# A fused attention and FFN kernel: more of the exponential on VectorE, with other places for the FFN product and the last head

## What is computed

```
x = x + attention(layernorm(x))
  q = x Wq^T  (4 query groups x 8 heads x 16),  k, v = x Wk^T, x Wv^T  (8 heads x 16)
  a_dot = softmax(q k^T / sqrt(16)) v            # full, over the 2048 tokens of the batch
  sigma = elu(q);  a_mem = sigma memory / (sigma memory_norm)
  out   = a_dot (1 - w) + a_mem w,   w = sigmoid(memory_weight)
x = x + ffn(layernorm(x))
  x_q = float8(clip(x / s)) * s;   out = x_q (weight * weight_scale)^T      # 512 x 512
```

## Time and profile before

| | |
|---|---|
| median of 3 runs | 2017.57 us (2016.67 to 2018.4) |
| the profiled execution's own time | 2018.72 us |
| its span, first to last instruction | 2017.0 us |
| ACT busy | 1876.7 us (93%) |
| PE busy | 1736.2 us (86%) |
| DVE busy | 1529.7 us (76%) |
| mean granted TensorE clock | 0.992 |
| DMA | 128 MB, 64 GB/s |

### The profile page before, as it was taken

One profiled execution on the slowest core, in us unless ns is written; L12 is line 12 of the kernel. 1 busy time (PEld: TensorE's weight loads), 2 busy tenths in 40 slices (PEclk: granted clock), 3 DMA queues, 4 the chain that ended last, 5 costly groups with the idle time before them and its releaser, 6 DMA issues.

```text
span 2017.0 us, 77616 instructions
## 1 busy us (share of the span) xinstructions
PE 1736.2 (86%) x35884; PEld 664.5 (33%) x35892; DVE 1529.7 (76%) x1746; ACT 1876.7 (93%) x2100; POOL 99.5 (5%) x148
## 2 busy tenths in 40 slices
PE   8997788888888888888888888888888888888887
PEld 7883222222222222222222222222222222222225
DVE  7664687778777788778777788777877778877856
ACT  5555899999999999999999999999999999999996
POOL 5540000000000000000000000000000000000000
PEclk9998899999999999999999999999999999999999
DMA  6563111111122211212111211121111211121111
GB/s 230 198 199 104 40 39 50 50 42 51 37 53 53 74 40 45 53 56 59 40 50 53 74 48 36 53 73 43 48 40 53 74 53 39 46 74 45 49 39 45
DMA packets 131500, 128.37 MB, mean 64 GB/s; under 512 B 30518, under 2 KB 106726, under 8 KB 131174
## 3 DMA queue, kind: packets, MB, share of 16 engines
q1 hardware_dynamic: 130166, 121.55, 20.7%
q10 hardware_dynamic: 1008, 1.84, 0.3%
HBM read 87.36 MB, written 32.24 MB: 59 GB/s over the span
## 4 chain that ended last, share of the span: by engine, by line
ACT 64%; PE 19%; DVE 12%; issue 3%; DMA 1%; POOL 1%; SPq 0%; ACTq 0%; DVEq 0%; POOLq 0%
ACT pool L825 64%; PE ps L904 6%; PE ps L989 5%; PE ps L1105 5%; DVE late L1540 3%; DVE v_tiles L1546 3%; DVE late L1532 2%; DVE late L1537 2%; PE ps L1144 2%; PE ps L1203 1%; DVE y_out L1649 1%; PE ps L877 1%; DVE late L1544 0%; PE ps L1188 0%; DMA resid<-in_x 0%
## 5 line engine op out<-in xcount | busy, mean ns | idle before, releaser
L825 ACT ACTIVATE pool<-ps 128x1024 f32<-128x1024 f32 x1892 | 1752.6, 1121 | 44.9 <-PE ps L989 39.6
L1105 PE MATMUL ps<-pool,v_st 64*32 64x512 f32 x16128 | 1063.5, 593 | 11.4 <-issue 8.0
L989 PE MATMUL ps<-q_st,k_st 51*32 51x512 f16 x16128 | 770.4, 383 | 248.7 <-ACT pool L825 219.1
L989 PEld LDWEIGHTS ps<-q_st,k_st 51*32 51x32 f16 x16128 | 228.8, 90 | 1098.2 <-ACT pool L825 841.8
L1105 PEld LDWEIGHTS ps<-pool,v_st 64*32 64x32 f32 x16128 | 289.1, 106 | 134.4 <-issue 49.7
L1532 DVE TENSOR_SCALAR late<-ps 128x1024 f32<-128x1024 f32 x124 | 151.7, 1224 | 171.1 <-PE ps L989 171.1
L1562 DVE STREAM_TRANSPOSE by_token<-ps 128x512 f32<-128x512 f32 x126 | 82.5, 693 | 123.2 <-PE ps L1105 123.2
L1556 DVE SCALAR_TENSOR_TENSOR pool<-late 128x2048 f32<-128x2048 f32 x62 | 142.1, 2292 | 11.8 <-PE ps L1105 9.8
L1540 DVE SCALAR_TENSOR_TENSOR late<-late 128x2048 f32<-128x2048 f32 x62 | 142.1, 2292 | 2.1
L1553 DVE SCALAR_TENSOR_TENSOR late<-late,v_tiles 128x2048 f32<-128x2048 f32 x62 | 142.1, 2292 | 2.1
L1551 DVE SCALAR_TENSOR_TENSOR late<-v_tiles 128x2048 f32<-128x2048 f32 x62 | 141.8, 2286 | 1.2
(11 more groups left out here) (169 smaller groups left out, 1011.9 us busy)
## 6 DMA issues: line engine op xcount, KB each, us to landing
q_st<-q_aug SPq DMA_DIRECT2D x128, 128.0 KB
k_st<-k_aug SPq DMA_DIRECT2D x128, 128.0 KB
v_st<-v_aug SPq DMA_DIRECT2D x64, 256.0 KB, 3.0
sigma_kept<-y_out SPq DMA_DIRECT2D x32, 256.0 KB, 2.0
q_aug<-parts SPq DMA_DIRECT2D x32, 256.0 KB, 2.7
q_st<-q_aug SPq DMA_DIRECT2D x128, 64.0 KB
k_st<-k_aug SPq DMA_DIRECT2D x128, 64.0 KB
wqT<-sigma_kept SPq DMA_DIRECT2D x32, 256.0 KB, 3.0
```

What stands on the lines that cost most here:

```text
L825: act.activation(held[:, half_u * 2 * CH:half_u * 2 * CH + 2 * CH], sc[slot_of("exp", unit)].rearrange("p a b -> p (a b)"), ACT.Exp, scale ...
L989: last = pe.matmul(dst[VW * c:VW * c + VW, x, :], k_st[RT * x:RT * x + AUG, par, keys:keys + VW], q_st[RT * x:RT * x + AUG, par, q * CH:q ...
L1105: last = pe.matmul(acc[r][VW * c:VW * c + VW, :].rearrange("v (i s) -> v i s", s=VW), v_st[rows, par, j, :], by_place[rows, c, :, :], star ...
```

## The change

1. **One unit more per head goes from ACT to DVE.** In heads 1 to 62, ACT has 29 units and DVE three, six strips of 512: the late tile as before, and the second half of the tile before it (`EXTRA_TILE`). The third unit is scored at unit 24 of an even head or 22 of an odd one, and the first two at 11 and 12, or 8 and 9. It has a chain of its own, `late_extra_strips`, behind `late_end`, into the buffer `late_extra`. Its last step waits until every tile of head n has been weighed.
2. **Another exponential on DVE.** The scores are taken as 32-bit integers in fixed point; two bitwise steps split them into exponent and mantissa, and four float32 steps make the polynomial. Before, it was two cheap steps and five float32 steps.
3. **The FFN product** goes from unit 19 of an odd head to unit 2 of the next even head, `ffn_out` to the front of DVE's call, and in the last head to unit 1 (before, 6). The turn of the FFN weight goes from unit 20 to 15.
4. **The last head without row tiles.** Its scores and its weighing use all 128 rows with 4 column positions, over operands whose unused rows are zero: POOL clears `k_st` at the start and half of `q_st` before the last head, one copy of q and k is loaded, each token tile has one bank of `acc` and DVE one transpose.
5. **First stores.** SP issues the last store of `v_tiles` before it waits for the guard rows, and DVE waits for it in the first `late_end` only.
6. ACT adds a bias column (`lift`) in the exponential.

```
-LATE_AT = (11, 12)
+LATE_AT = ((11, 12, 24), (8, 9, 22))
-WEIGHT_TURN_AT = 20
-PRODUCT_AT = 19
-LAST_PRODUCT_AT = 6
+WEIGHT_TURN_AT = 15
+PRODUCT_AT = 2
+LAST_PRODUCT_AT = 1
...
+def late_units(n):
+    if not 0 < n < LAST_HEAD:
+        return 0
+    return LATE + 1
+
 def exp_units(n):
     if n == LAST_HEAD:
         return LAST_UNITS
-    return 2 * ST if n == 0 else 2 * LATE_TILE
+    return 2 * ST - late_units(n)
...
+            if a == PRODUCT_AT and product_tile(n) is not None:
+                turns.append(("product", product_tile(n)))
             if a == MEMORY_AT:
                 turns.append(("memory", n // 2))
...
+            def take_late(n, x, place):
+                number = LATE_BASE[n] + x
+                dve.wait_ge(late_scores, number + 1)
+                dve.tensor_scalar(late_x[:, place * 2 * CH:(place + 1) * 2 * CH].bitcast(I32),
+                                  sc[slot_of("late", number)].rearrange("p a b -> p (a b)"),
+                                  -2.0 ** 23 / OCTAVE, LOWEST, ALU.mult, ALU.min).then_inc(late_taken, 1)
+
+            def chain_begin(step, width):
+                fixed, part = late_x[:, 0:width], late_z[:, 0:width]
+                dve.tensor_scalar(part.bitcast(I32), fixed.bitcast(I32), MANTISSA, QUARTER,
+                                  ALU.bitwise_and, ALU.bitwise_or).then_inc(late_step, 1)
+                dve.wait_ge(late_step, step + 1)
+                dve.tensor_scalar(fixed.bitcast(I32), fixed.bitcast(I32), EXPONENT, ONE,
+                                  ALU.bitwise_and, ALU.bitwise_xor).then_inc(late_step, 1)
+                dve.scalar_tensor_tensor(part, part, POWER[0], part, ALU.add, ALU.mult).then_inc(late_step, 1)
+
+            def chain_end(step, width, dst, weighed=0):
+                power, part, grown = late_x[:, 0:width], late_z[:, 0:width], late_y[:, 0:width]
+                dve.wait_ge(late_step, step + 3)
+                dve.scalar_tensor_tensor(grown, part, POWER[1], part, ALU.add, ALU.mult).then_inc(late_step, 1)
+                dve.wait_ge(late_step, step + 4)
+                dve.scalar_tensor_tensor(grown, grown, POWER[2], part, ALU.add, ALU.mult).then_inc(late_step, 1)
+                dve.wait_ge(late_step, step + 5)
+                if weighed:
+                    dve.wait_ge(pv_done, weighed)
+                return dve.scalar_tensor_tensor(dst, grown, POWER[3], power, ALU.add, ALU.mult)
...
             def late_end(n):
+                if n == 1:
+                    for par in range(2):
+                        dve.wait_ge(v_stored[par], 16 * (NG // 2 + 1))
+                else:
+                    dve.wait_ge(pv_done, late_weighed(n - 1))
+                chain_end(chains_before(n) * CHAIN_STEPS, LATE * 2 * CH, late_probs).then_inc(late_ready, 1)
+
+            def late_extra_strips(n):
+                step = (chains_before(n) + 1) * CHAIN_STEPS
+                dve.wait_ge(late_ready, n)
+                take_late(n, LATE, 0)
+                dve.wait_ge(late_taken, LATE_BASE[n] + LATE + 1)
+                chain_begin(step, 2 * CH)
+                chain_end(step, 2 * CH, late_extra[:, :], (n - 1) * ST + ST if n > 1 else 0).then_inc(late_extra_ready, 1)
...
             def head(n):
                 g, h = divmod(n, HEADS)
+                if product_tile(n) is not None:
+                    ffn_out(*divmod(product_tile(n), TPC))
                 if n > 0:
                     add_head(n - 1)
...
-                if n % 2 == 1:
-                    if n // 2 == WEIGHT_PAIR:
-                        copy_ffn_weight()
-                    elif g > 0:
-                        ffn_out(g - 1, h // 2)
-                if has_late(n + 1):
+                if n % 2 == 1 and n // 2 == WEIGHT_PAIR:
+                    copy_ffn_weight()
+                if late_units(n + 1):
                     late_end(n + 1)
+                if late_units(n + 1) > LATE:
+                    late_extra_strips(n + 1)
...
-            for par in range(2):
-                dve.wait_ge(v_stored[par], 16 * (NG // 2 + 1))
             for n in range(LAST_HEAD):
                 head(n)
```

On PE, tile 14 is then weighed in two halves of 256 columns, the second one out of `late_extra`, and the last head loses its row positions:

```
+                if late_units(n) > LATE and j == EXTRA_TILE:
+                    half_places = QG * TPC // 2
+                    weigh(n, j, held[:, 0:2 * CH], slice(0, half_places))
+                    pe.wait_ge(late_extra_ready, n)
+                    last = weigh(n, j, late_extra[:, :], slice(half_places, 2 * half_places), last_tile=last_tile)
...
-                for c in range(P // VW):
-                    for x in range(ROW_TILES):
+                by_tile = q_st[:, 1, :].rearrange("r (q t s) -> r t q s", q=QG, t=TPC)[:, t, :, :]
+                for x in range(2):
+                    for c in range(P // VW):
                         keys = (2 * pair + x) * P + c * VW
...
+                        last = pe.matmul(sc[slot_of("exp", unit)][VW * c:VW * c + VW, x, :], k_st[:, 1, keys:keys + VW], by_tile,
+                                         start=True, stop=True)
```

More of the change, by code:

```diff
@@ L57 @@
 LATE_TILE = ST - 1
+EXTRA_TILE = ST - 2
 LATE = 2
@@ L79, in exp_units, with late_at, product_tile @@
         return LAST_UNITS
-    return 2 * ST if n == 0 else 2 * LATE_TILE
-def has_late(n):
-    return 0 < n < LAST_HEAD
+    return 2 * ST - late_units(n)
+def late_at(n):
+    return LATE_AT[n % 2][0:late_units(n + 1)]
+def product_tile(n):
+    tile = n // 2 - FIRST_PRODUCT_PAIR - 1
+    return tile if n % 2 == 0 and tile >= 0 else None
 def slot_turns(n):
@@ L89, in slot_turns @@
     for a in range(exp_units(n)):
-        if a in LATE_AT and has_late(n + 1):
-            turns.append(("late", LATE * n + LATE_AT.index(a)))
+        if a in late_at(n):
+            turns.append(("late", LATE_BASE[n + 1] + late_at(n).index(a)))
         if n == LAST_HEAD:
@@ L95, in slot_turns @@
         elif n % 2 == 0:
+            if a == PRODUCT_AT and product_tile(n) is not None:
+                turns.append(("product", product_tile(n)))
             if a == MEMORY_AT:
                 turns.append(("memory", n // 2))
-        elif n // 2 == WEIGHT_PAIR:
-            if a == WEIGHT_TURN_AT:
-                turns.append(("weight", 0))
-        elif n // 2 >= FIRST_PRODUCT_PAIR:
-            if a == PRODUCT_AT:
-                turns.append(("product", n // 2 - FIRST_PRODUCT_PAIR))
+        elif n // 2 == WEIGHT_PAIR and a == WEIGHT_TURN_AT:
+            turns.append(("weight", 0))
         turns.append(("exp", EXP_BASE[n] + a))
     return turns
+LATE_BASE = [sum(late_units(m) for m in range(n)) for n in range(LAST_HEAD + 2)]
 EXP_BASE = [sum(exp_units(m) for m in range(n)) for n in range(LAST_HEAD + 2)]
@@ L647, in _ @@
             pool_e.memset(ones_row[:, :], 1.0 / GUARD_UNIT).then_inc(ones_set, 1)
+            pool_e.memset(k_st[:, :, :].rearrange("p a s -> p (a s)").bitcast(F32), 0.0).then_inc(keys_cleared, 1)
+            pool_e.memset(lift[:, :], LIFT).then_inc(ones_set, 1)
             pool_e.wait_ge(ones_set, 2)
@@ L704, in _, with rstd_of_tiles @@
             bound_roots(1)
-            with pool_e.Fori(0, NT) as i:
-                pool_e.wait_ge(f_eps, i + 1)
-                pool_e.tensor_tensor(rstd[:, 0, 0:1], var_eps[:, 0:1], minus_half[:, 0:1], ALU.pow).then_inc(f_rstd, 1)
-                pool_e.wait_ge(f_rstd, i + 1)
+            def rstd_of_tiles(first, end):
+                with pool_e.Fori(first, end) as i:
+                    pool_e.wait_ge(f_eps, i + 1)
+                    pool_e.tensor_tensor(rstd[:, 0, 0:1], var_eps[:, 0:1], minus_half[:, 0:1], ALU.pow).then_inc(f_rstd, 1)
+                    pool_e.wait_ge(f_rstd, i + 1)
+            rstd_of_tiles(0, (NG - 1) * TPC - 1)
+            pool_e.wait_ge(scores_ready, EXP_BASE[LAST_HEAD - 1])
+            pool_e.wait_ge(f_rstd, (NG - 1) * TPC - 1)
+            pool_e.memset(q_st[:, 1, :].bitcast(F32), 0.0).then_inc(last_cleared, 1)
+            pool_e.wait_ge(last_cleared, 1)
+            rstd_of_tiles((NG - 1) * TPC - 1, NT)
             pool_e.wait_ge(xq_ready, NT)
@@ L820, in _ @@
                     j, half_u = divmod(a, 2)
-                    held = late_probs if j == LATE_TILE else probs[:, j % RING, :]
+                    held = probs[:, probs_place(n, j), :]
                     act.wait_ge(scores_ready, unit + 1)
                     act.activation(held[:, half_u * 2 * CH:half_u * 2 * CH + 2 * CH],
-                                   sc[slot_of("exp", unit)].rearrange("p a b -> p (a b)"), ACT.Exp, scale=EXP_UNIT / SCORE_UNIT)\
+                                   sc[slot_of("exp", unit)].rearrange("p a b -> p (a b)"), ACT.Exp, bias=lift[:, :],
+                                   scale=EXP_UNIT / SCORE_UNIT)\
                         .then_inc(probs_ready, 1)
@@ L1104, in weigh @@
                         rows = slice(RT * r, RT * r + RT)
[L1105 to L1106 removed]
+                        last = pe.matmul(acc[r][VW * c:VW * c + VW, :].rearrange("v (i s) -> v i s", s=VW)[:, places, :],
```

(8 more changed lines are left out.)

176 lines of the change are left out of this document (85 added, 91 removed).

## The result

The changed kernel takes **2360.77 us** (median of 4 runs, 2359.47 to 2362.49) where the kernel before takes 2017.63 in the same session: a ratio of 1.1701, interval 1.1681 to 1.1722. The forecast was 2285 and the range ended at 2360, so the sign and the kind of the mechanism held, and 76 us of the size were missed. The profiled run took 2359.82 us, its span is 2357.5.

A forecast was written before the change was run, and what follows sets the result against it. ACT bounds the kernel before; DVE becomes the bound: 56.8 us work, 6.0 waits and 3.1 for the clock make 65.9 a period. Over all periods +284.0, with start -13.5 and end -3, 2285 us; range 2110 to 2360.

The forecast's parts named there:

- VectorE's work: DVE's steps in a two-head period: 45.8 us plus 10.6 net for the third unit, 56.4 (walked with 56.8).
- The waits: Four places where DVE still waits at full clock: takes, last extra step, memory products; 6.0 us a period, making 62.8.
- My walk: Step-by-step timing of one period from the odd head's transposes, all clocks full: 56.8 us work, 6.0 waits, ending at 62.8.
- The clock: PE idles 4.9 us before the odd head's transposes, falls to half rate, delays the takes: 3.1 us a period, giving 65.9.
- two falls: Rival: clock also falls at the product's gap, delaying memory products and takes; period 69.2 us, 2345 to 2372 us; 8%.
- the clock holds: Rival: same waits but no fall of PE's clock, period 62.8 us, 2189 us; 20%.
- The bias: nothing: ACT's exponential with one more column of 4 bytes: nothing, at most 0.02 us a unit, hidden by DVE.
- The ends: First heads: ACT's early stalls mostly go, -13.5 us (-8 to -16); last head without row tiles, -3 (-6 to +3).
- The product's new place: PE makes the moved FFN product, 1.0 us, before unit 2's scores and tile 14, inside the last extra step's 2.5 us wait.
- The sum: Periods between first and last odd transposes total 2030.7 us, +284.0; with both ends +267.5, against the median 2285 us.
- fewer waits: Rival: DVE is the bound but waits only 1 to 4 us a period; 2032 to 2125, up to 2150 us; 14%.
- DVE keeps up: Rival: ACT stays the bound, period 54.5 us, 1942 us, or 2001 with DVE at 56.4 and no wait; 7%.

The follow-up runs named there:

- the third run of part 3: Changed kernel, bias column kept, with 14 extra makings of scores on TensorE in every odd head, ahead of the first weighing: 2262.08 us (ratio 1.1215).
- those with the filler: Six-strip kernels with 14 extra, overwritten makings of scores in odd heads: 2260.89 us with immediate bias, 2262.08 with the column; with 32 further small products 2258.10.

## Why the prediction was right or wrong

One period, term by term; the last column is the changed kernel without a fall (the third run of part 3):

| us a period | forecast | after | after, no fall |
|---|---|---|---|
| VectorE's work | 56.8 | 56.4 | 56.6 |
| takes of the odd head, and the step behind them | 1.4, and 3.1 for the clock | 3.7 | 1.2 |
| last extra step, odd head | 2.5 | 3.9 | 3.9 |
| last extra step, even head | 0 | 0.2 | 0.2 |
| memory products | 1.45 | 2.8 | 1.7 |
| takes of the even head | 0.6 | 1.2 | 1.2 |
| together | 65.9 | 68.3 | 64.85 |

- **VectorE's work: right.** 1.224 us for the take, 0.69 for a bitwise step and 1.22 to 1.23 for a float32 step of 1024 columns, as interpolated from the earlier trace rows. It is the bound: with the bias column or without it the period is the same, 68.26 with the falls of the clock and 64.85 without those that cost.
- **The waits: right in kind and place, mis-sized by 2.2 us a period** (walked 6.0, found 8.2 at full clock). The step that failed is, above all, the wait of the extra chain's last step in the odd head: forecast 2.5 us, measured 3.9, which is 1.4 of the 2.2. The takes of the even head are 0.6 more (1.2 for 0.6), the memory products and the even head's last step 0.2 each, less 0.2 at the odd head's takes. My walk had unit 28 ending 23.65 us after the transposes; it ends 1050.34 - 1023.28 = 27.1 us after them in the trace. About 1.7 us of that are units that start every 1.01 us and not every 0.926, and 1.9 the later start of unit 7 (4.7 in place of 2.75) behind the fallen clock. With the immediate bias and no fall the wait is 3.07, so 0.6 us of its miss was my margin, and 0.9 the column. But the column does not make the period longer: without it the even head's last step waits 1.56 us, with it 0.23. That wait I had at nothing.
- **The clock: right in size for the whole, by luck, wrong in number.** 3.4 us a period were found, 3.1 forecast. But there are two falls, not one: 2.5 us of waits at the takes, as reasoned from the stall before 222.88 (I had 3.1), and 1.2 us at the product's gap, which I had given 3.3 us and 8%. The rival *two falls* gave 2345 to 2372 and so had the right time, but with nearly three times the price for its second fall, in place of the waits that were missing. The rival *the clock holds* (2189) is answered by 2262: it is out, and its own sum lacked the same 2.2 us a period.
- **"The bias: nothing" was the plain error.** It costs 0.09 us a unit, not 0.02 at most. It was saved by luck: hidden by VectorE here (1 to 8 us), 126 to 136 us where ScalarE is the bound. The trace of the kernel before could have shown it. Its exponential has no column, but two other activations out of PSUM have one for their scale (L771 and L845, with `scalars`), and take 0.08 and 0.09 us more than one of the same size without (L771 writes in another layout):

```profile
L845 ACT ACTIVATE y_out<-ps,scalars 128x512 f32<-128x512 f32 x1 | 0.7, 688 | 2.1 <-PE ps L1237 2.1
L771 ACT ACTIVATE v_tiles<-ps,scalars 128x512 f32<-128x512 f32 x8 | 5.4, 676 | 1.8 <-PE ps L943 1.8
L765 ACT ACTIVATE v_turn<-ps 128x512 f32<-128x512 f32 x8 | 4.8, 598 | 15.5 <-PE ps L904 15.5
```

  The Trainium skill (ScalarE: Activation LUTs, What ACT_TABLE_LOAD costs) gives 93 ns for each pointer operand of an activation; the runs agree, with a median of 0.996 us from start to start with the column and 0.903 without. The prediction did not weigh that sentence.
- **The ends: the first heads right, the last head too small.** -12.7 us in the first heads (forecast -13.5), -6.7 in the last (forecast -3, bound -6): its 32 units idle ACT for 0.7 us in place of 5.1, and the tail behind it shortened too. Without the column it is -9.5.
- **The product's new place, costed inside the walk at 1.0 us ahead of tile 14:** 0.8 us, but given back behind it.
- **The sum.** From transposes of head 0 to those of head 62 I had 2030.7 us; it is 2106.7. First chunk 198.2 for 194; the period without a product 67.6 for 64.2; 26 periods of 68.3 for 65.9, which is 63 us of the miss; the last 64.6 for 59.3: together 76 us, from which the ends took back 3. The range ended 0.8 us too low: it cut the rival with two falls in its middle, and that rival stood on the walked waits. Their uncertainty, some 2 us a period, I had used downwards only (*fewer waits*), never upwards.
- *DVE keeps up* and *fewer waits* fell, with no period under 64.6. Of my signs: DVE over 90% busy was wrong (78%), and the forecast's own 56.8 us of work in 65.9 did not allow it; the extra step waited 3.9 us, not 2.5, and the clock fell twice a period, not once; ACT at 80% came out as 84 because of the column; the stalls at unit 6 (4.4) and unit 4 (1.1) are as said.

**Left open.** The changed kernel, the one with the immediate and the one with the product put back have the same period of 68.26 us, to 0.01, though their waits are distributed differently and their clocks read 0.93, 0.90 and 0.92; so have the two kernels with two buffers (61.45), and those with the filler (64.85). In the kernel with the product put back, one wait lost 0.82 us and two others gained 0.84. The three values stand 3.4 us apart. My walk would give each kernel its own period. No run here tells why they settle on these.

## What to carry to other kernels

Idle time of an engine is also the cover of every release that depends on it. When work fills it, add to the work each wait of a fixed order that used to end early, above all one that waits for the last reader of a single buffer: here 8.2 us a period, of which a second buffer gave back 3.4; that is 108 us, and 178 with the falls of the clock that hung on it. And compare each operand of the instruction that the bound engine repeats: one column in place of a constant cost 6%.

## What was new about the hardware

- An activation of 128x1024 out of PSUM with a column as its bias: 0.996 us from start to start (median), with an immediate 0.903. In the kernel before, an activation of 128x512 with a column as its scale took 0.688 us, one without 0.598.
- A fall of TensorE's clock to 1.2 GHz (the two of the changed kernel came around gaps of TensorE of 4.49 and 1.93 us) cost time only where VectorE waited for what TensorE made in it: 2.5 us ahead of the takes, nothing at the third take of the even head (with two buffers the same period at 0.94 and 1.00), and 22 us in all where it lay ahead of the takes in the kernel with two buffers. Fourteen needless makings of scores in every second head saved 92 to 99 us, 4% of the kernel. The Trainium skill (TensorE: Matmul & The Clock Gate, Part 1) puts the penalty of the ramp at under 1% of a typical span, in a passage on a kernel's first matmuls; in this kernel the falls come in every period, and the measurement decides otherwise.
